# Routed experts in slots of two experts with 64 rows each, their weights copied ahead, in place of slots of one expert with 128 rows

## The chip, the cores and the metric

The kernel runs on one core of one Trainium2 chip. The metric is device time in microseconds of one execution of the whole program, as the median of several runs. The program is one block of instructions for each of the five engines (TensorE or PE, VectorE or DVE, ScalarE or ACT, GpSimd or POOL, and SyncE or SP, which only issues DMAs), tied together by semaphores written by hand.

## The reference

A stack of layers over an input of 4 x 512 tokens of 128 features, all fp32: a linear recurrence, two layers of local attention with a gated feed-forward, a global attention with 8 heads, and last a mixture of experts. Only the last part is touched. With 2048 tokens `x`, 32 experts of hidden size 256 and a shared expert:

```
chosen = the expert with the highest gate logit of the token (one per token), score s
h      = normed token, scaled by s
routed = (silu(h @ Wg[chosen]) * (h @ Wu[chosen])) @ Wd[chosen]     # 128 -> 256 -> 128
out    = x + shared_expert(normed token) + routed
```

How many tokens an expert gets is known only when the kernel runs, so rows are sorted by expert on the chip.

## The kernel before, in words

**Sorting.** VectorE counts the tokens of each expert, and gives each expert as many tiles of P = 128 rows as it needs. `ntile` is the number of tiles (a comparison of the count with 0, 128, 256, ..., one column for each of the TILES = 16 possible tiles, on 32 x 16 = 512 elements, L1191, and its sum, L1193), `incl` its running sum, `base_e` the first tile of each expert. From these comes `slot_i`, the row of `xs_dram` of each token, and semaphore `slots` releases POOL, which scatters the 16 tiles of 128 token rows (129 values: 128 features and the token's number) with 16 indirect DMAs (L645). A table `exp_of` then names the expert of each tile (L1209 and L1211, on one partition, 52 x 32 = 1664 elements). Meanwhile the shared expert runs on TensorE, ScalarE and VectorE; its last add (L1110) brings semaphore `x4s` to 4. `xs_dram` was filled with zeros earlier, in one DMA beside the first layers.

**The slots.** In the worst case there are 16 + 31 = 47 tiles, rounded to LOOP_TILES = 48 slots; all are always run. Slots run in a software pipeline: `experts` emits four slots, a hardware loop (`Fori`) of 10 passes with four slots, and four more; so semaphore targets and addresses in the loop come from registers. Slot j does this:

- SP loads its 128 rows from `xs_dram` into one of four buffers, `rows_in` (L508, `refill`). A refill waits for the transposition of the tile that was in the buffer and for its number.
- POOL takes the token numbers out of the rows (`number`, L653) into `slot_id`. Empty rows are sent to one of four spare rows of `y_dram`.
- PE transposes the rows (`tokens_T`, L1596), ACT brings them to SBUF (`tokens_sb`, L839).
- PE reads the expert's number into a register (`expert_of`, L1599, a value load out of `exp_of`), then multiplies: rows stationary, the expert's gate and up weights moving, 512 columns, straight out of `wgu`, in which all 32 experts lie (`gate_up`, L1603). An fp32 matmul is two instructions here.
- ACT makes Silu of the gate half (`gate_sb`, L845), DVE multiplies it with the up half (`gated`, L1222).
- PE transposes the product in two pieces (`gated_T`, L1609), ACT brings it back (`back_sb`, L851), PE multiplies it with the down weights in `wd` (`down`, L1616, two matmuls of 128 columns).
- DVE copies the result to `ys` (L1231), and POOL scatters its 128 rows to their places in `y_dram` with one indirect DMA (L670). Before the number of slot j+2, POOL waits until the scatter of slot j-2 has landed (`ys_out`).

On each engine the stages are offset: in step j PE does gate-up of j+2, the tokens' transposition of j+3, the product's transposition of j+1 and down of j.

**The end.** SP waits for the scatters, gathers `y_dram` in token order in four DMAs, DVE adds them (L1240), SP writes the output.

Of the kernel before, what the change touches and what calls it, by code (L numbers as in the profile page):

```python
# [8 lines left out]
I32 = mybir.dt.int32  # L9
U32 = mybir.dt.uint32  # L10
ALU = mybir.AluOpType
# [3 lines left out]
P = 128  # L15
# [52 lines left out]
def build(nc, A, out):  # L68
    with ExitStack() as ctx:
# [137 lines left out]
        m3 = region_r[0:1, 3072:3072 + (LOOP_TILES + AHEAD) * EXP]  # L207
# [11 lines left out]
        exp_of_f = region_b[0:1, 8800:8800 + LOOP_TILES + AHEAD]  # L219
        exp_of = region_b[0:1, 8864:8864 + LOOP_TILES + AHEAD].bitcast(I32)  # L220
# [12 lines left out]
        def bank(n, width=BANK, of=1):  # L233
# [20 lines left out]
            "sp_turn", "pool_turn", "ids", "xT_mm", "xT_sb", "gu_mm", "r_silu", "r_act", "actT_mm", "actT_sb", "y_mm", "y_sb", "x4")}  # L254
# [4 lines left out]

        def experts(engine, step):  # L260


            for r in range(AHEAD):
                step(0, r, False)
            with engine.Fori(1, PASSES - 1) as i:
                for r in range(AHEAD):
                    step(i, r, False)
            for r in range(AHEAD):
                step(PASSES - 1, r, True)
# [119 lines left out]
        def _(sp):  # L389
# [110 lines left out]
            def refill(t, j):  # L500

                sp.wait_ge(M["xT_mm"], j + 1)
                if not isinstance(j, int):
                    sp.sem_inc(M["sp_turn"], 1)
                sp.wait_ge(M["ids"], j + 1)
                if not isinstance(j, int):
                    sp.sem_inc(M["sp_turn"], 1)
                sp.dma_start(rows_in[t], xs_dram[bass.ds((j + AHEAD) * P, P), :]).then_inc(xs_in[t], 16)  # L508

            def sp_step(i, r, last):  # L510
                if not last:
                    refill((r + NUM) % AHEAD, i * AHEAD + r + NUM)

            for t in range(NUM):
                refill(t, t)
            experts(sp, sp_step)
            for r in range(AHEAD):
                sp.wait_ge(ys_out[r], 16 * PASSES)
# [7 lines left out]
            for r in range(AHEAD):  # L526
                sp.wait_ge(xs_in[r], 16 * (PASSES + (r < NUM)))
# [4 lines left out]
        def _(pool):  # L532
# [115 lines left out]
            def number(t, i):  # L648
# [7 lines left out]
            for t in range(NUM):  # L656
                number(t, 0)
# [1095 lines left out]
```

## Time and profile before

| | |
|---|---|
| runs | 841.93 us median of 3 (841.46 to 844.74) |
| the profiled execution | 842.27 us |
| its span, first to last instruction | 840.5 us |
| mean granted TensorE clock | 0.920 of full speed |
| PE busy / weight loads busy | 664.2 us (79%) / 396.8 us (47%) |
| DVE / ACT / POOL busy | 518.7 (62%) / 374.4 (45%) / 323.9 us (39%) |
| DMA | 50.57 MB, mean 60 GB/s |
| the chain that ended last | PE 48%, DVE 19%, issue 14%, DMA 7%, ACT 7%, POOL 3% |

Busy time is the time in which an engine had at least one instruction in execution; register, branch and semaphore instructions are not in it. They run on an engine's queue and are named with a q (`PEldq`). The chain that ended last goes back from the last instruction, at each step to what released it; "issue" in it is time in which nothing in the profile was waited for. A timeline row gives start, duration, engine, line and operation, out<-in and a count, and in brackets how long the engine had been idle and what ended that.

### The profile page before, as it was taken

What the parts mean: (1) busy time and instruction counts of PE and PEld (TensorE: products, weight loads), DVE (VectorE), ACT (ScalarE), POOL (GpSimd) and SP (SyncE); (2) the same over time, 40 slices, a digit from 0 to 9 for tenths busy, and PEclk for the clock granted to TensorE, in tenths of its full rate; (3) what the DMA queues carried; (4) which work ended last, traced back from release to release, by engine and by line L of the source; (5) the groups of instructions that cost most, each with busy time, mean ns of one, the idle gap of its engine ahead of it and who ended that gap; (6) DMA issues with size and microseconds to landing.
All of it is one profiled execution on the core that took longest, in us unless ns stands there. A gap on an engine that the chain in (4) does not pass through costs nothing.

```text
span 840.5 us, 14653 instructions
## 1 busy us (share of the span) xinstructions
PE 664.2 (79%) x5076; PEld 396.8 (47%) x5078; DVE 518.7 (62%) x915; ACT 374.4 (45%) x602; POOL 323.9 (39%) x318
## 2 busy tenths in 40 slices
PE   3566899999998999999775555789888966888881
PEld 2244666566656656665553232123233544455551
DVE  7647998778778777877733256866763553222222
ACT  0113446756575564657443542254656521333330
POOL 4544556454454445546311063200001017355552
PEclk8659999999999999999998966689999988899996
DMA  8103210100010010001000137636326101122224
GB/s 253 28 13 117 81 27 21 27 21 13 21 28 18 16 27 14 20 21 27 15 1 1 45 79 154 152 100 143 109 79 229 49 4 47 49 62 60 59 60 119
DMA packets 35507, 50.57 MB, mean 60 GB/s; under 512 B 5965, under 2 KB 24697, under 8 KB 34169
## 3 DMA queue, kind: packets, MB, share of 16 engines
q1 hardware_dynamic: 33401, 45.58, 20.9%
q0 software_dynamic: 2048, 4.21, 1.5%
q8 instruction: 38, 0.62, 0.3%
q14 instruction: 20, 0.16, 0.1%
HBM read 30.31 MB, written 11.83 MB: 50 GB/s over the span
## 4 chain that ended last, share of the span: by engine, by line
PE 48%; DVE 19%; issue 14%; DMA 7%; ACT 7%; POOL 3%; SPq 1%; POOLq 0%; DVEq 0%; ACTq 0%
PE ps L1603 5%; PE ps L1397 5%; DVE region_b L965 5%; DVE smx L962 5%; PE ps L1351 4%; PE ps L1337 4%; PE ps L1308 4%; PE ps L1328 3%; DVE mneg L1139 3%; PE ps L1405 3%; PE ps L1461 3%; DMA region_b<-parts_dram 2%; PE ps L1616 2%; ACT pts L723 2%; PE ps L1545 2%
## 5 line engine op out<-in xcount | busy, mean ns | idle before, releaser
L567 POOL TENSOR_TENSOR rnorm<-ssum_c,neg_half 128x16 f32<-128x16 f32 x32 | 93.8, 2932 | 157.0 <-DVE ssum_c L935 157.0
L1139 DVE TENSOR_REDUCE mneg<-ps 128x2 f32<-128x1024 f32 x64 | 75.3, 1217 | 33.1 <-PE ps L1532 33.1
L579 POOL TENSOR_TENSOR region_r<-region_b,region_d 128x512 f32<-128x512 f32 x64 | 80.8, 1283 | 30.3 <-DVE region_b L940 29.5
L813 ACT ACTIVATE region_r<-ps 128x1024 f32<-128x1024 f32 x64 | 64.4, 1024 | 54.2 <-PE ps L1545 54.1
L545 POOL TENSOR_TENSOR var_eps<-mv,eps 128x4 f32<-128x4 f32 x20 | 5.0, 250 | 184.4 <-DVE mv L878 184.4
L1222 DVE TENSOR_TENSOR region_r<-region_r,ps 128x256 f32<-128x256 f32 x48 | 20.2, 422 | 77.0 <-ACT region_r L845 45.5
L670 POOL DMA_INDIRECT y_dram<-region_r x48 | 50.0, 1043 | 44.3 <-DVE region_r L1231 25.9
L1603 PE MATMUL ps<-region_a,region_r 128*128 x96 | 55.4, 660 | 13.2 <-issue 12.5
L684 ACT ACT_TABLE_LOAD x49 | 62.9, 1283 | 1.6 <-PEq L1745 0.7
L699 ACT ACTIVATE region_a<-ps 128x1024 f32<-128x1024 f32 x32 | 33.0, 1032 | 63.0 <-PE ps L1295 63.0
L1397 PE MATMUL ps<-region_a,region_d 128*114 128x512 f32 x96 | 49.4, 640 | 12.8 <-ACT region_a L717 8.6
L992 DVE SCALAR_TENSOR_TENSOR region_b<-ps,b,region_a 114x512 f32<-114x512 f32 x24 | 18.0, 751 | 53.5 <-ACT region_a L747 53.5
L962 DVE TENSOR_REDUCE smx<-ps 128x8 f32<-128x1024 f32 x32 | 39.2, 1224 | 15.7 <-PE ps L1328 15.3
L1337 PE MATMUL ps<-ident,region_b 128*128 128x128 f32 x256 | 35.0, 280 | 15.3 <-DVE region_b L965 15.3
L1337 PEld LDWEIGHTS ps<-ident,region_b 128*128 128x128 f32 x256 | 27.4, 141 | 40.0 <-DVE region_b L965 40.0
L1294 PE MATMUL ps<-region_d,hT 128*128 128x512 f32 x64 | 36.1, 648 | 11.0 <-DVE region_b L940 7.8
L716 ACT ACTIVATE region_a<-ps 128x512 f32<-128x512 f32 x32 | 19.1, 597 | 57.3 <-PE ps L1308 57.3
L839 ACT ACTIVATE region_r<-ps 128x128 f32<-128x128 f32 x48 | 13.3, 278 | 70.0 <-PE ps L1596 70.0
L932 DVE TENSOR_REDUCE ssum<-region_a 128x16 f32<-128x1024 f32 x32 | 38.8, 1213 | 9.2 <-ACT region_a L699 9.2
L1351 PE MATMUL ps<-region_b,pts 128*64 128x65 f32 x512 | 36.6, 226 | 8.6 <-ACT pts L723 8.5
L940 DVE TENSOR_TENSOR region_b<-ps,rnorm 128x1024 f32<-128x1024 f32 x32 | 39.0, 1218 | 6.0 <-POOL rnorm L567 6.0
L1532 PE MATMUL ps<-region_b 96*128 96x512 bf16 x96 | 34.0, 451 | 9.4 <-DMA region_b<-parts_dram 4.4
(214 smaller groups left out, 1549.9 us busy)
## 6 DMA issues: line engine op xcount, KB each, us to landing
region_a<-in_wgu SPq DMA_DIRECT2D x16, 512.0 KB, 3.7
region_b<-region_a SPq DMA_DIRECT2D x56, 130.0 KB, 2.3
region_d<-in_wd SPq DMA_DIRECT2D x4, 1024.0 KB, 5.8
xs_dram<-region_a SPq DMA_DIRECT2D x1, 3354.0 KB, 12.9
pts<-xs_dram SPq DMA_DIRECT2D x50, 64.5 KB
parts_dram<-region_b SPq DMA_DIRECT2D x8, 384.0 KB, 2.6
region_b<-parts_dram SPq DMA_DIRECT2D x6, 384.0 KB, 6.9
region_d<-in_wqkv SPq DMA_DIRECT2D x2, 768.0 KB, 8.6
```

Of the source, the lines that this page charges most:

```text
L567: g.tensor_tensor(rnorm[:, :], ssum_c[n % 2][:, :], neg_half[:, :], ALU.pow).then_inc(S["rnormed"], 1)
L579: g.tensor_tensor(dst, src, tab, ALU.mult).then_inc(S["rot_bb"], 1)
L670: g.indirect_dma_start(out=y_dram[:, :], out_offset=bass.IndirectOffsetOnAxis(ap=slot_id[:, r:r + 1], axis=0), in_=ys[r], in_offset=None). ...
L684: act_(warm[:, :], ones_f[:, 0:1], function).then_inc(S["warm"], 1)
L813: act_(dst, bank(l1_bank[what, b, i], of=2), ACT.Exp).then_inc(T["ex"], 1)
L962: d.tensor_reduce(smx[n % 2][:, :], sc, AX.X, ALU.max).then_inc(S["smax"], 1)
L965: d.tensor_tensor(sdiff[n % 2], sc, smx[n % 2][:, :].unsqueeze(2).to_broadcast([P, HEADS, P]), ALU.subtract).then_inc(S["diffed"], 1)
L1139: d.tensor_reduce(mneg[b % 2][:, 2 * i:2 * i + 2], bank(l1_bank[what, b, i], of=2) .rearrange("p (q t) -> p q t", q=2), AX.X, ALU.max, neg ...
L1337: last = tr(bank(6 + h // 4)[:, (h % 4) * P:(h % 4 + 1) * P], sdiff[n % 2][:, h, :], ident[:, :])
L1351: last = mm(ps[w * WIN:(w + 1) * WIN, c0:c0 + VW], pts[n % 2][:, j, w * WIN:(w + 1) * WIN], vals[:, t, h, :], start=True, stop=True)
L1397: last = mm(ps[0:HW, (6 + g) * BANK:(7 + g) * BANK], w1[k // BATCH][:, g, c, :], hnT, start=True, stop=True)
L1603: mm(bank(2 + t % 2), xsT[t % 2], wgu[:, bass.ds(e, 1), :].rearrange("p a n -> p (a n)"), start=True, stop=True).then_inc(M["gu_mm"], 1)
```

## The change

The unit of sorting becomes HALF = 64 rows. HALVES = 32 is the largest number of halves of an expert, and with 31 more for the split ones there are 63, in PAIRS = 32 slots of two halves, which may belong to two experts. All 32 are unrolled, so targets and addresses are constants, but for the expert's number.

- Sorting: the comparison and its sum run over 32 x 32 = 1024 elements, the table over 64 x 32 = 2048. `xs_dram` has 4096 rows instead of 6656.
- Per slot DVE copies the gate-up weights of the first expert and the down weights of both into SBUF buffers (`weights_one`), ACT copies the gate-up weights of the second (`weights_two`). Three buffers for gate-up, four for down. DVE reads two expert numbers per slot, ACT one; PE reads none.
- PE: `gate_up` is two matmuls, each with 64 of the slot's rows stationary and its own expert's 512 columns moving, into partitions 0 to 63 and 64 to 127 of one bank; `down` is four of 128 columns in the same manner.
- DVE and ACT wait for `slots`, `x4s` and the weights before the first copies; PE's own waits for them go (all but `x4s`).
- POOL, SP: the same steps without the loop.

```diff
-SLOT_TILES = TILES + EXP - 1
-AHEAD = 4
-LOOP_TILES = -(-SLOT_TILES // AHEAD) * AHEAD
-PASSES = LOOP_TILES // AHEAD
-UP, XT, BACK, NUM = 2, 3, 1, 2
-SLOT_ROWS = (LOOP_TILES + AHEAD) * P
+HALF = P // 2
+HALVES = TOK // HALF
+PAIRS = -(-(HALVES + EXP - 1) // 2)
+AHEAD, NUM, GBUF, DBUF = 4, 2, 3, 4
+SLOT_ROWS = PAIRS * P
...
+            for j in range(PAIRS - AHEAD):
                 sp.wait_ge(M["xT_mm"], j + 1)
                 sp.wait_ge(M["ids"], j + 1)
+                sp.dma_start(rows_in[j % AHEAD], xs_dram[(j + AHEAD) * P:(j + AHEAD + 1) * P, :]).then_inc(xs_in[j % AHEAD], 16)
...
+            def number(j):
+                pool.wait_ge(xs_in[j % AHEAD], 16 * (j // AHEAD + 1))
+                if j >= AHEAD:
+                    pool.wait_ge(ys_out[j % AHEAD], 16 * (j // AHEAD))
+                g.tensor_scalar(slot_id[:, j % AHEAD:j % AHEAD + 1], rows_in[j % AHEAD][:, P:ROW], float(j % AHEAD), None,
                                 ALU.max).then_inc(M["ids"], 1)
+            for j in range(PAIRS):
+                if j + NUM < PAIRS:
+                    number(j + NUM)
+                pool.wait_ge(M["ids"], j + 1)
+                pool.wait_ge(M["y_sb"], j + 1)
                 g.indirect_dma_start(out=y_dram[:, :],
...
+            def expert_two(j):
+                return a.value_load(exp_of[0:1, 2 * j + 1:2 * j + 2], min_val=0, max_val=EXP - 1)
+            def weights_two(j, e):
+                need(a, M["gu_mm"], j - GBUF + 1)
+                act_(gu_pair[j % GBUF][1], wgu[:, bass.ds(e, 1), :].rearrange("p a n -> p (a n)"), ACT.Copy)\
+                    .then_inc(M["w_two"], 1)
...
+            for j in range(PAIRS):
+                if j + 3 < PAIRS:
+                    weights_two(j + 3, e)
+                if j + 4 < PAIRS:
+                    e = expert_two(j + 4)
+                if j + 2 < PAIRS:
+                    gate_sb(j + 2)
+                if j + 3 < PAIRS:
+                    tokens_sb(j + 3)
+                if j + 1 < PAIRS:
+                    back_sb(j + 1)
...
-            link(d.tensor_tensor(m1.rearrange("p (e k) -> p e k", e=EXP), cnt.unsqueeze(2).to_broadcast([P, EXP, TILES]),
-                                 consts[:, EXP:EXP + TILES].unsqueeze(1).to_broadcast([P, EXP, TILES]), ALU.is_gt))
+            link(d.tensor_tensor(over, cnt.unsqueeze(2).to_broadcast([P, EXP, HALVES]),
+                                 consts[:, EXP:EXP + HALVES].unsqueeze(1).to_broadcast([P, EXP, HALVES]), ALU.is_gt))
...
+            def experts_of(j):
+                return [v.value_load(exp_of[0:1, 2 * j + w:2 * j + w + 1], min_val=0, max_val=EXP - 1) for w in range(2)]
+            def weights_one(j, pair):
+                need(v, M["gu_mm"], j - GBUF + 1)
+                d.tensor_copy(gu_pair[j % GBUF][0], wgu[:, bass.ds(pair[0], 1), :].rearrange("p a n -> p (a n)"))
+                need(v, M["y_mm"], j - DBUF + 1)
+                for w in range(2):
+                    last = d.tensor_copy(d_pair[j % DBUF][w], wd[:, bass.ds(pair[w], 1), :, :].rearrange("p a c n -> p (a c n)"))
+                last.then_inc(M["w_one"], 1)
...
+            v.wait_ge(M["slots"], 2)
+            v.wait_ge(M["x4s"], BATCH)
+            v.wait_ge(M["w_gu"], 16 * 16)
+            v.wait_ge(M["w_d"], 4 * 16)
+            for j in range(3):
+                weights_one(j, experts_of(j))
+            pair = experts_of(3)
+            gated(0)
+            gated(1)
+            for j in range(PAIRS):
+                if j + 3 < PAIRS:
+                    weights_one(j + 3, pair)
+                if j + 4 < PAIRS:
+                    pair = experts_of(j + 4)
+                if j + 2 < PAIRS:
+                    gated(j + 2)
+                routed_sb(j)
...
+            def gate_up(j):
+                pe.wait_ge(M["xT_sb"], j + 1)
+                pe.wait_ge(M["w_one"], j + 1)
+                pe.wait_ge(M["w_two"], j + 1)
+                for w in range(2):
+                    rows = slice(w * HALF, (w + 1) * HALF)
+                    last = mm(bank(2 + j % 2)[rows, :], xsT[j % 2][:, rows], gu_pair[j % GBUF][w], start=True, stop=True,
+                              skip_group_check=True)
+                last.then_inc(M["gu_mm"], 1)
...
+            def down(j):
+                pe.wait_ge(M["actT_sb"], j + 1)
+                need(pe, M["y_sb"], j - 1)
                 for c in range(IC):
+                    for w in range(2):
+                        at = c * P + w * HALF
+                        last = mm(bank(6 + j % 2)[w * HALF:(w + 1) * HALF, 0:P], actT[j % 2][:, at:at + HALF],
+                                  d_pair[j % DBUF][w][:, c * P:(c + 1) * P], start=(c == 0), stop=(c == IC - 1),
+                                  skip_group_check=True)
```

## Rows read from the trace of the kernel before

**Rows 1.** The chain of waits from 640 us on: start, duration, what.
```profile
714.34 2.11 DMA pts<-xs_dram
...
717.48 2.07 PE ps L1603 x2
...
817.22 3.26 DMA y_dram<-region_r
...
827.53 3.10 DMA y_dram<-region_r
```

**Rows 2.** Groups from 700 us on: count | busy us, mean ns | idle before, releasers.
```profile
L1603 PE MATMUL ps<-region_a,region_r 128*128 x96 | 55.4, 660 | 13.2 <-issue 12.5 <-ACT region_r L839 0.5
L670 POOL DMA_INDIRECT y_dram<-region_r x48 | 50.0, 1043 | 44.3 <-DVE region_r L1231 25.9 <-issue 10.5 <-DMA y_dram<-region_r 4.9
...
L1222 DVE TENSOR_TENSOR region_r<-region_r,ps 128x256 f32<-128x256 f32 x48 | 20.2, 422 | 77.0 <-ACT region_r L845 45.5 <-issue 22.2 <-PE ps L1609 9.3
...
L845 ACT ACTIVATE region_r<-ps 128x256 f32<-128x256 f32 x48 | 18.1, 378 | 2.4 <-PE ps L1603 2.4
...
L1231 DVE COPY region_r<-ps 128x128 f32<-128x128 f32 x48 | 13.6, 284 | 1.3 <-issue 0.8 <-PE ps L1616 0.5
...
L839 ACT ACTIVATE region_r<-ps 128x128 f32<-128x128 f32 x48 | 13.3, 278 | 70.0 <-PE ps L1596 70.0
```

**Rows 3.** Timeline of TensorE, 784 to 800 us.
```profile
787.48 1.12 PE L1603 MATMUL ps<-region_a,region_r 128*128 x2 [0.36 <-issue]
788.44 0.27 PE L1596 MATMUL ps<-ident,pts 128*128 128x128 f32 x1
...
788.76 0.61 PE L1616 MATMUL ps<-region_d,region_r 128*128 x4
789.21 1.07 PE L1603 MATMUL ps<-region_a,region_r 128*128 x2
...
797.92 1.07 PE L1603 MATMUL ps<-region_a,region_r 128*128 x2
```

**Rows 4.** All instructions of line 1599 (the value load): duration ns min/median/max.
```profile
L1599 PEldq FUSED_REGOPS  x122: 46/151/165, 717.0 to 820.0; - x122
L1599 PEldq TENSOR_LOAD <-region_b x72: 296/303/498, 716.5 to 819.6; - x72
```

**Rows 5.** Timeline of POOL, 700 to 840 us.
```profile
725.37 1.05 POOL L670 DMA_INDIRECT y_dram<-region_r  x1 [8.24 <-DVE region_r L1231]
...
820.77 0.21 POOL L653 TENSOR_SCALAR region_r<-pts 128x1 uint32<-128x1 f32 x1 [0.65 <-DMA y_dram<-region_r]
821.61 1.05 POOL L670 DMA_INDIRECT y_dram<-region_r  x1 [0.62 <-issue]
```

**Rows 6.** Timeline of TensorE in the two attentions, matmuls on array quarters and halves.
```profile
559.67 1.07 PE L1461 MATMUL ps<-region_r,pts 128*32 128x512 f32 x8
560.66 0.60 PE L1532 MATMUL ps<-region_b 96*128 96x512 bf16 x2
...
304.56 0.24 PE L1351 MATMUL ps<-region_b,pts 128*64 128x65 f32 x1 [0.42 <-ACT pts L723]
...
305.49 0.22 PE L1351 MATMUL ps<-region_a,pts 128*64 128x65 f32 x1
```

**Rows 7.** All instructions of lines 986 and 803, copies within SBUF.
```profile
L986 DVE COPY region_b<-y x4: 293/295/296, 113.7 to 354.4; 128x256 f32<-128x256 f32 x4
...
L803 ACT ACTIVATE region_b<-pts x8: 629/629/630, 493.6 to 534.7; 128x512 bf16<-128x512 f32 x8
```

**Rows 8.** Timeline of VectorE, 684 to 726 us.
```profile
685.84 0.69 DVE L1193 TENSOR_REDUCE region_b<-region_r 128x32 f32<-128x512 f32 x1
...
696.00 1.87 DVE L1209 TENSOR_TENSOR region_r<-region_r,region_b 1x1664 f32<-1x1664 f32 x1
...
714.57 0.69 DVE L1110 TENSOR_TENSOR xr<-xr,ps 128x512 f32<-128x512 f32 x1 [4.82 <-remote]
720.38 0.42 DVE L1222 TENSOR_TENSOR region_r<-region_r,ps 128x256 f32<-128x256 f32 x1 [5.13 <-ACT region_r L845]
```

More of the change, by code:

```diff
@@ L258, in build @@
         block = ctx.enter_context(nc.Block())
[L260 to L269, printed above, removed]
         def l1_steps():
@@ L498, in _ @@
                 sp.dma_start(rows_in[r], xs_dram[r * P:(r + 1) * P, :]).then_inc(xs_in[r], 16)
-            def refill(t, j):
+            for j in range(PAIRS - AHEAD):
                 sp.wait_ge(M["xT_mm"], j + 1)
-                if not isinstance(j, int):
-                    sp.sem_inc(M["sp_turn"], 1)
                 sp.wait_ge(M["ids"], j + 1)
[L506 to L516, printed above, removed]
+                sp.dma_start(rows_in[j % AHEAD], xs_dram[(j + AHEAD) * P:(j + AHEAD + 1) * P, :]).then_inc(xs_in[j % AHEAD], 16)
             for r in range(AHEAD):
-                sp.wait_ge(ys_out[r], 16 * PASSES)
+                sp.wait_ge(ys_out[r], 16 * (PAIRS // AHEAD))
             for b in range(BATCH):
@@ L832, in _, with tokens_sb @@
                 silu(n)
[L834 removed]
+            def expert_two(j):
[4 more added lines that the diff above has]
+                    .then_inc(M["w_two"], 1)
+            def tokens_sb(j):
                 a.wait_ge(M["xT_mm"], j + 1)
[L837 to L839 removed]
@@ L841, in gate_sb @@
-            def gate_sb(t, j):
+                need(a, M["gu_mm"], j - 1)
+                act_(xsT[j % 2], bank(j % 2)[:, 0:P], ACT.Copy).then_inc(M["xT_sb"], 1)
+            def gate_sb(j):
                 a.wait_ge(M["gu_mm"], j + 1)
-                if not (isinstance(j, int) and j < 2):
-                    a.wait_ge(M["r_act"], j - 1)
-                act_(silu_r[t % 2], bank(2 + t % 2)[:, 0:INTER], ACT.Silu).then_inc(M["r_silu"], 1)
-            def back_sb(t, j):
+                need(a, M["r_act"], j - 1)
+                act_(silu_r[j % 2], bank(2 + j % 2)[:, 0:INTER], ACT.Silu).then_inc(M["r_silu"], 1)
@@ L848, in back_sb @@
+            def back_sb(j):
                 a.wait_ge(M["actT_mm"], j + 1)
-                if not (isinstance(j, int) and j < 2):
-                    a.wait_ge(M["y_mm"], j - 1)
-                act_(actT[t % 2], bank(4 + t % 2)[:, 0:INTER], ACT.Copy).then_inc(M["actT_sb"], 1)
-            def act_step(i, r, last):
-                for lag, do in ((XT, tokens_sb), (UP, gate_sb), (BACK, back_sb)):
-                    if not last or r + lag < AHEAD:
-                        do(r + lag, i * AHEAD + r + lag)
@@ L858, in _ @@
-            for t in range(XT):
-                tokens_sb(t, t)
-            for t in range(UP):
-                gate_sb(t, t)
-            back_sb(0, 0)
-            experts(a, act_step)
+                need(a, M["y_mm"], j - 1)
+                act_(actT[j % 2], bank(4 + j % 2)[:, 0:INTER], ACT.Copy).then_inc(M["actT_sb"], 1)
+            a.wait_ge(M["slots"], 2)
+            a.wait_ge(M["x4s"], BATCH)
+            a.wait_ge(M["w_gu"], 16 * 16)
+            weights_two(0, expert_two(0))
+            tokens_sb(0)
@@ new lines, in down @@
+                last.then_inc(M["y_mm"], 1)
+            pe.wait_ge(M["x4s"], BATCH)
+            tokens_T(0)
+            tokens_T(1)
+            gate_up(0)
+            tokens_T(2)
+            gate_up(1)
+            gated_T(0)
+            for j in range(PAIRS):
+                if j + 2 < PAIRS:
+                    gate_up(j + 2)
+                if j + 3 < PAIRS:
+                    tokens_T(j + 3)
+                if j + 1 < PAIRS:
+                    gated_T(j + 1)
+                down(j)
```

125 lines of the change are left out of this document (38 added, 87 removed).

## The prediction

> **What bounds the kernel now.** I read the chain of waits first, then the groups of instructions of the last stage, then timelines of single engines. The chain says what the end hangs on: the row loads out of `xs_dram` land at 716.5 us, then TensorE is the chain for most of the stage, then the scatters of the expert rows to `y_dram`, whose last one is under way from 827.53 for 3.10 us, then the four gathers and adds [rows 1]. So the part that the change rewrites runs from 716.5 to 830.6 us: 114 us for 48 slots. All before 690 us, and the last 9.9 us (830.6 to 840.5), are untouched.
>
> In that stage no engine is full: POOL's 48 scatters take 50.0 us, TensorE's gate-up matmuls 55.4 us, VectorE and ScalarE under half of the time [rows 2]. The matmul timeline shows the rhythm: gate-up starts at 789.21 and, four slots on, at 797.92, 2.18 us a slot. A slot without idle takes 1.73 us (787.48 to 789.21: 0.96 for gate-up, 0.32 for three transposes, 0.45 for down) [rows 3]. The other 0.45 us are TensorE's queue: it reads the expert's number into a register 72 times in 48 slots, with a TENSOR_LOAD of 0.303 us each and 122 register operations of 0.151 [rows 4]: 0.303 + 122/72 x 0.151 = 0.56 us a load, about 0.6 with the gaps, 1.5 loads a slot, partly hidden behind matmuls.
>
> POOL stands just behind. A scatter starts only when the one two slots earlier has landed: starts at 817.22 and 821.61 [rows 1, 5], a ring of 4.39 us for two slots, 2.2 us a slot. In it are 3.26 us until the data has landed, 0.29 until the number of a later slot starts at 820.77, and 0.84 from there to the next scatter. So two limits of 2.2 us a slot lie on each other, and the measured 2.18 shows that the coupling of the engines adds nothing visible.
>
> **Part 1, 32 slots for 48.** Every slot still moves 128 rows in and 128 rows out. Sixteen of them go. At today's 2.18 that is -34.9 us. What matters now is the new length p of a slot.
>
> **Part 2, TensorE.** Its value loads all go. Gate-up becomes two fp32 matmuls of 512 columns, each with 64 rows stationary on one half of the array's columns; down becomes four of 128 columns for two. Do the halves run beside each other? Two rows say yes. In the attention, four fp32 matmuls of 512 columns, each on a quarter (`128*32 128x512 f32 x8`, two instructions each), go by in 0.99 us (559.67 to the next start at 560.66), where a single full-width one takes 0.96. And the 32 instructions on halves of L1351 start within 0.93 us, 304.56 to 305.49, 0.03 us each [rows 3, 6]. So a slot stays at 0.96 + 0.32 + 0.45 = 1.73 us. The changes between whole and half array, twice a slot, have no clean row; bound 0 to 0.2 each (idle of that size would still show in rows 6), I take 0.1: TensorE needs 1.9, between 1.7 and 2.2.
>
> **Part 3, VectorE.** It copies one expert's gate-up weights (128x512) and both down weights (128x256 each) in every slot, beside its product (0.422) and its eviction (0.284) [rows 2]. The nearest row for a copy within SBUF is L986, 128x256 in 0.295, against 0.422 for a product of the same size: a copy runs at well above the product's rate [rows 2, 7]. Estimate for 128x512: 0.295 + 256 x 0.52 ns (half of the 1.05 that 0.69 and 0.422 us for 512 and 256 elements make) = 0.43; lower end that, upper end 0.69 (the one-element rate of L1193 [rows 8]). Sum 0.43 + 2 x 0.295 + 0.422 + 0.284 = 1.73, with 0.2 for the gaps of five instructions 1.9 us. It also does two value loads a slot, 1.2 us of its queue. They stand behind the three copies, which are issued first and run for 1.02 us meanwhile; then comes the product, which needs the gate's Silu anyway. Hidden fully: 1.9. Not hidden at all: 3.1. I take 2.1, since TensorE's queue hides most of its loads the same way. New waits of VectorE (gate-up of j, down of j-1) name work that is done before its previous eviction, and cost nothing; if they were late, gate-up of the next slot would be.
>
> **Part 4, ScalarE.** One copy of 128x512; the nearest row, SBUF to SBUF, is L803 with 0.629 [rows 7]; with Silu 0.378, the other 128x256 eviction about the same and 0.278 [rows 2] it is 1.66 us a slot plus one value load, mostly beside it: 1.7 to 2.3. In front of nothing critical; if it lost its cover, Silu and so VectorE's product would be late.
>
> **Part 5, POOL and SP.** Same scatter, same number, same waits in the same order: the ring of 2.2 us stays (the lesser register work is worth nothing inside a ring made of a landing). SP's refill waits on the same two events, and a load is asked for four slots ahead.
>
> So TensorE 1.9, VectorE 2.1, ScalarE 2.0, ring 2.2. I start from p = 2.2 and add a third of the price below for POOL being disturbed: **p = 2.35**.
>
> What a row shows first: the copies of L986 take 0.295 us where a one-element rate gives 0.422 [rows 2, 7], and no row has POOL start a scatter beside one. The Trainium skill, "SBUF — State Buffer", "SBUF: two separate sides", says that such an fp32 SBUF-to-SBUF copy of VectorE shuts GpSimd off its shared port, so that it can't write the descriptors of its own DMAs. By that rule the ring would stretch as the second rival works out; without it p is 2.2. No run here shows it yet.
>
> **Part 6, before the loop.** "More than" over 1024 elements instead of 512, and its sum: L1193 takes 0.69 for 512 and L1222 0.422 for 256 [rows 8, 2], so 1.22 for 1024, +0.53 each, +1.1 us ahead of the row scatters and of the shared expert. The expert table grows from 1664 to 2048 elements: L1209's 1.87 becomes 2.3, and its sum likewise, +0.9. Both lie ahead of the shared expert's last add on VectorE (714.57 [rows 8]), whose chain with TensorE and ScalarE has no slack; it ends 1.9 us later, at 717.2. Only then do the copies begin: two value loads (1.2) and three copies (1.1), so the first weights stand at 719.5, where gate-up started at 717.5 (its chain row [rows 1]). VectorE then prepares slots 1 and 2 and reads pair 3 (three times about 1.6) before the first product: at 724.4 instead of 720.38 [rows 8]. The first scatter follows 5.0 us after the first product today [rows 5, 8], with three slow gate-ups on the way (the first took 2.07 us [rows 1]); they are done by then, so I take it at 729 instead of 725.37 (+3.6, bounds +2 and +6). Zeroing less of `xs_dram` lies beside the layers, worth nothing.
>
> **The sum.** First scatter 729.0; 31 more starts at p; last landing 3.1; tail 9.8: a span of 741.9 + 31p. At p = 2.35 that is 814.8. The profiled execution was 842.27 us at a span of 840.5, 1.8 outside it: **816.5 us**. The median of the three runs (841.93) is 0.3 below the profiled one, less than I can tell. The span equals today's at p = 3.18; 0.5% (4.2 us), about what this measurement can tell from no change, is reached at p = 3.03 and 3.30.
>
> **Rivals.**
> 1. Leaner than thought, p of 2.05 to 2.15 (two scatters of the ring overlap better once the row latencies fall): 807 to 810 us. Chance 0.08. Against it: the ring is a landing, which the change does not touch.
> 2. VectorE's copies disturb POOL. POOL's part of the ring that could be stopped is number, start-up and descriptor work, 0.84 + 1.04 = 1.9 us in two slots; a copy runs 1.02 of every 2.2 us, so about 0.46 of it falls on copies, 0.9 us in two slots, p = 2.65: 825.9 us. With part of the value loads exposed on top, up to p = 3.0 and 837 us. For it: the copies are certain and POOL's ring has no slack. Against it: VectorE copies right after its eviction, while POOL needs some 0.75 us before its scatter starts, so much of the lock would fall in a pause. Chance 0.20.
> 3. VectorE's value loads take the place of TensorE's. If its queue does not read registers while its copies run, each slot costs 1.9 + 2 x 0.6 = 3.1 us, and 3.4 with 0.75 a load. Time 839.8 to 849: the other side of today. It decides from a slot of 3.18 us on. Against it: TensorE has slots of 1.73 us without idle, with a load inside [rows 3]. No change 0.05, slower 0.05 (the next one's share is in neither).
> 4. The halves do not run beside each other, so the change doubles TensorE's work instead of sharing it: 1.92 + 0.32 + 0.90 = 3.14 us a slot, 3.3 with the mode changes: 841 to 846 us. [rows 6] speak against it. Chance 0.02.
>
> **How the numbers follow.** The forecast, p between 2.15 and 2.55 (810 to 823 us), has 0.60. Faster by over 0.5%: 0.60 + 0.08 + 0.20 = 0.88; within 0.5% 0.05; slower 0.05 + 0.02 = 0.07. The range goes from 808 (rival 1 in large part) to 834 (rival 2 but for its end); it leaves out some 0.17.
>
> **What would show it.** 32 scatters with starts 2.2 to 2.5 us apart, and 4.4 or more for two; TensorE's two gate-up halves starting together, next start within 1.1 us; VectorE copies near 0.43 and 0.295 (0.69 would mean that the fast copy is not in use); its value loads in the copies' shadow; the first scatter near 729. A scatter instruction longer than 1.05 us, or the 0.84 us before it grown, shows rival 2; VectorE idle for "issue" before its product shows rival 3; gate-up of 1.9 us shows rival 4. I am wrong if p is outside 2.15 to 2.55, or if the first scatter comes after 731.

## The result and the profile after

| | before | after |
|---|---|---|
| median of four runs | 842.42 us (841.46 to 844.74) | 804.56 us (803.24 to 806.3) |
| profiled execution, span | 842.27, 840.5 us | 806.3, 804.5 us |

The ratio is 0.9547, with an interval of 0.9523 to 0.957: 38 us or 4.5% faster. The prediction said 816.5 us, 808 to 834. So the direction was right and the size too small; the result lies 3.4 us below the range.

The page of the kernel after, its span and first part:

```profile
span 804.5 us, 14011 instructions
...
PE 640.2 (80%) x5125; PEld 369.6 (46%) x5125; DVE 532.3 (66%) x979; ACT 378.5 (47%) x586; POOL 309.2 (38%) x286
```

Its groups from 700 us on (columns as in rows 2):

```profile
L1613 PE MATMUL ps<-region_b,region_r 128*64 128x512 f32 x128 | 35.0, 626 | 0.0
L639 POOL DMA_INDIRECT y_dram<-region_r x32 | 33.2, 1039 | 20.2 <-DVE region_r L1226 9.9 <-POOL region_r L629 9.7 <-issue 0.6
L1630 PE MATMUL ps<-region_b,region_r 128*64 128x128 f32 x256 | 20.9, 285 | 0.0
L807 ACT ACTIVATE region_b<-region_a 128x512 f32 x32 | 19.9, 622 | 6.6 <-DVE xr L1096 6.2 <-issue 0.4
...
L1214 DVE COPY region_b<-region_d 128x256 f32 x64 | 15.8, 287 | 0.0
L1220 DVE TENSOR_TENSOR region_r<-region_r,ps 128x256 f32<-128x256 f32 x32 | 13.5, 421 | 19.5 <-issue 9.9 <-PE ps L1620 6.3 <-ACT region_r L819 3.2
L1211 DVE COPY region_b<-region_a 128x512 f32 x32 | 13.4, 420 | 3.3 <-issue 3.3
...
L629 POOL TENSOR_SCALAR region_r<-pts 128x1 uint32<-128x1 f32 x32 | 12.4, 387 | 6.5 <-DMA pts<-xs_dram 3.8 <-issue 0.9 <-DMA y_dram<-region_r 0.9
```

Gate-up, which in [rows 2] had 13.2 us of idle time in front of it, now has 0.0: TensorE is never idle just before gate-up or down. The matmul timeline of the kernel after shows a rhythm without a gap:

```profile
758.00 1.03 PE L1613 MATMUL ps<-region_b,region_r 128*64 128x512 f32 x4
758.96 0.33 PE L1604 MATMUL ps<-ident,pts 128*128 128x128 f32 x1
759.12 0.38 PE L1620 MATMUL ps<-ident,region_r 128*128 128x128 f32 x2
759.43 0.66 PE L1630 MATMUL ps<-region_b,region_r 128*64 128x128 f32 x8
759.92 1.03 PE L1613 MATMUL ps<-region_b,region_r 128*64 128x512 f32 x4
```

From start to start: 0.96 for both halves of gate-up (one expert alone took 0.96 before), 0.47 for three transposes (0.32 in [rows 3]), 0.49 for both halves of down (0.45), 1.92 us a slot. POOL keeps up with it; its timeline (the answer to [rows 5]):

```profile
732.24 1.05 POOL L639 DMA_INDIRECT y_dram<-region_r  x1 [7.49 <-DVE region_r L1226]
...
757.80 1.04 POOL L639 DMA_INDIRECT y_dram<-region_r  x1 [0.36 <-POOL region_r L629]
758.88 0.60 POOL L629 TENSOR_SCALAR region_r<-pts 128x1 uint32<-128x1 f32 x1
759.67 1.04 POOL L639 DMA_INDIRECT y_dram<-region_r  x1 [0.20 <-POOL region_r L629]
760.75 0.59 POOL L629 TENSOR_SCALAR region_r<-pts 128x1 uint32<-128x1 f32 x1
761.54 1.05 POOL L639 DMA_INDIRECT y_dram<-region_r  x1 [0.20 <-POOL region_r L629]
...
784.14 0.41 POOL L629 TENSOR_SCALAR region_r<-pts 128x1 uint32<-128x1 f32 x1 [0.42 <-DMA y_dram<-region_r]
```

Two slots take 3.74 us here (757.80 to 761.54) where [rows 1, 5] gave a ring of 4.39, and the number at 760.75 starts without a wait for the scatter of 757.80. Only near the end (784.14 and 788.24) does the profile name a landing as what POOL waits for. Three more numbers (743.71, 753.08 and 776.48) follow 0.3 us of idle time that is put down to issue, and each starts 3.2 us behind a scatter with 107 to 115 empty rows (counted as told under "The landing"); these were probably short waits for a landing too. The end of the chain of waits:

```profile
791.56 3.10 DMA y_dram<-region_r
...
796.26 4.68 DMA region_b<-y_dram
```

**Where the time went.** Each profile can be cut at three events of POOL's timeline: the first row scatter (into `xs_dram`), the first result scatter (into `y_dram`) and the last one. The table gives the first, the distance to the second, the mean spacing of the result scatters, and what follows after the last one starts.

| profile | span | first row scatter | to first result scatter | spacing | last start to end |
|---|---|---|---|---|---|
| before | 840.5 | 691.40 | 33.97 | 2.174 x 47 | 13.0 |
| after | 804.5 | 698.41 | 33.83 | 1.913 x 31 | 12.9 |

So the profiled 36.0 us are made of: 16 slots fewer at the old spacing, -34.8; 31 spacings 0.26 shorter, -8.1; a start 7.0 us later; the rest -0.2 (rounded). The tail did not change. TensorE's granted clock is no part of the shorter spacing: it was 1.00 from 730 to 790 us in both profiles.

### The profile page after: what moved, and what is told of

Same layout as the page of the kernel before. It is cut to its first block, busy times and chain, and to the rows that moved or that the text cites. A ratio compares the mean times of both kernels' runs of the same rounds, so it can differ in the third digit from the quotient of the medians.

```text
span 804.5 us, 14011 instructions
## 1 busy us (share of the span) xinstructions
PE 640.2 (80%) x5125; PEld 369.6 (46%) x5125; DVE 532.3 (66%) x979; ACT 378.5 (47%) x586; POOL 309.2 (38%) x286
## 4 chain that ended last, share of the span: by engine, by line
PE 52%; DVE 19%; issue 12%; DMA 6%; ACT 6%; POOL 2%; SPq 1%; POOLq 0%; DVEq 0%; ACTq 0%
PE ps L1405 6%; DVE region_b L951 5%; DVE smx L948 5%; PE ps L1359 5%; PE ps L1345 4%; PE ps L1316 4%; PE ps L1336 4%; PE ps L1613 4%; PE ps L1469 3%; PE ps L1413 3%; DVE mneg L1125 3%; PE ps L1553 3%; DMA region_b<-parts_dram 2%; PE ps L1630 2%; ACT pts L690 2%
## 5 line engine op out<-in xcount | busy, mean ns | idle before, releaser
L1540 PE MATMUL ps<-region_b 96*128 96x512 bf16 x96 | 36.0, 471 | 14.5 <-DMA region_b<-parts_dram 9.7
L1359 PE MATMUL ps<-region_b,pts 128*64 128x65 f32 x512 | 36.5, 225 | 8.8 <-ACT pts L690 8.6
L690 ACT ACTIVATE pts<-ps 128x1024 f32<-128x1024 f32 x32 | 32.7, 1023 | 18.5 <-PE ps L1345 18.5
L639 POOL DMA_INDIRECT y_dram<-region_r x32 | 33.2, 1039 | 20.2 <-DVE region_r L1226 9.9
L1316 PE MATMUL ps<-ident,region_r 128*128 128x128 f32 x256 | 35.4, 283 | 6.2 <-DVE rot_b L888 6.2
L951 DVE TENSOR_TENSOR region_b<-ps,smx 128x1024 f32<-128x1024 f32 x32 | 39.2, 1224 | 1.1
```

The source lines that it names most:

```text
L690: act_(pts[n % 2].rearrange("p h q -> p (h q)"), bank(6, of=2), ACT.Exp).then_inc(S["exped"], 1)
L951: d.tensor_tensor(sdiff[n % 2], sc, smx[n % 2][:, :].unsqueeze(2).to_broadcast([P, HEADS, P]), ALU.subtract).then_inc(S["diffed"], 1)
L1316: last = tr(bank(6 + z)[:, h * P:(h + 1) * P], rot[n % 2][:, (z * HP + h) * P:(z * HP + h + 1) * P], ident[:, :])
L1359: last = mm(ps[w * WIN:(w + 1) * WIN, c0:c0 + VW], pts[n % 2][:, j, w * WIN:(w + 1) * WIN], vals[:, t, h, :], start=True, stop=True)
```

## The experiments

The texts put on record before each run use four letters. Two theories stood at first. **A**: TensorE's queue alone made the 2.18 us of the kernel before, and the scatter ring, read where the slots are empty, is shorter in the body; in the new kernel TensorE sets the slot. **B**, as predicted: the ring of 2.2 us a slot stands whatever TensorE does. Later two more came: **C**, the landing of a scatter depends on how many of its rows go to the same spare row of `y_dram`; and **D**, it has nothing to do with the destinations. Experiments on 48 slots start from the kernel before (b_), those on 32 slots from the kernel after (a_). All but the last two are single executions, beside one or more of the kernel before on the same chip; those of the kernel before alone lie between 841.5 and 845.8 us, so spacings tell more than times.

**b_noload: no value loads on TensorE, loop kept.**

```diff
-                return pe.value_load(exp_of[0:1, bass.ds(i * AHEAD + t, 1)], min_val=0, max_val=EXP - 1)
+                return 0
...
```

> The kernel before, in which TensorE reads no expert number: all 48 slots use expert 0 (left out: the choice of the weights). Theory A: before was bound by TensorE's queue alone, and the scatter ring of 4.39 us for two slots was read where the slots are empty; in the body it is shorter. Then a slot falls from 2.18 us to 1.75 to 1.9, and the span by 14 to 20 us. Theory B, as predicted: the ring of 2.2 us a slot stands whatever TensorE does. Then a slot stays at 2.15 to 2.2 us and the span within 2 us of before.

**b_unroll: the loop written out, the loads kept** (`for i in range(PASSES)` for the hardware loop).

> The kernel before with its hardware loop written out, all register loads kept (six for four slots). Theory A: the loads are what costs, the loop's branch and register arithmetic only a little: a slot of 2.05 to 2.15 us, the span 2 to 6 us less. Rival: the loop costs as much as the loads: a slot of 1.9 us, 13 us less. Theory B (ring of 2.2): nothing.

840.64 and 842.51 us, beside 845.81 for the kernel before. Spacings 2.084 and 2.113 for 2.174: taking every load away gives 0.09 us a slot, the loop alone 0.06. In b_noload the spacing lies between what A said (1.75 to 1.9) and what B said (2.15 to 2.2), so neither holds as it was put; b_unroll came out as A had it (2.05 to 2.15). Without the loads POOL's ring is the main limit. From b_noload, 730 to 826 us, the chain by line, and below it one of the waits (us in total, times, the longest):

```profile
by line: DMA y_dram<-region_r 57.6%; issue 25.2%; DMA pts<-xs_dram 5.8%; POOL region_r L653 3.8%; POOL y_dram L670 3.8%; DVE region_r L1231 1.2%; ACT region_r L845 1.2%; PE ps L1596 1.1%; POOLq L265 0.7%; POOLq L651 0.4%; POOLq L666 0.3%; P
```

```profile
POOL region_r L653 <- DMA y_dram<-region_r: 10.9, 18, 0.9
```

And its DMA issues from 730 to 770 us, with the median time from issue to landing at the end:

```profile
y_dram<-region_r POOLq DMA_INDIRECT x20, 3.0
```

A landing of 3.0 with 0.29 and 0.84 behind it (Part 5's terms) makes 4.1 for two slots, against 2 x 2.084 = 4.17 measured. So TensorE's queue was not the only limit: a ring close to the one of the prediction is there. But the kernel after runs at 1.92 with the same POOL code, so it has to have a shorter ring, and that needs a cause.

**a_serial: the first expert's rows full width.** In gate-up of the kernel after, the first matmul keeps all 128 rows stationary, so it can't run beside the second.

```diff
                     rows = slice(w * HALF, (w + 1) * HALF)
+                    if w == 0:
+                        rows = slice(0, P)
```

> The kernel after, but the first expert's gate-up is a full-width matmul over all 128 rows, and the second's overwrites the upper half; same results. The two can't run beside each other. If they do so in the kernel after, gate-up grows by its whole length, 0.86 us, a slot from 1.92 to 2.8, the span by some 27 us. If the halves ran one after the other anyway, or something other than TensorE set the slot, it grows by less than 0.3 us.

840.15 us, beside 845.81. Its matmul timeline:

```profile
759.20 2.13 PE L1615 MATMUL ps<-region_b,region_r 128*128 128x512 f32 x4
761.26 0.33 PE L1604 MATMUL ps<-ident,pts 128*128 128x128 f32 x1
761.43 0.38 PE L1622 MATMUL ps<-ident,region_r 128*128 128x128 f32 x2
761.74 0.66 PE L1632 MATMUL ps<-region_b,region_r 128*64 128x128 f32 x8
762.33 2.13 PE L1615 MATMUL ps<-region_b,region_r 128*128 128x512 f32 x4
```

Gate-up takes 2.06 for 0.96 and the slot 3.13 for 1.92, more than the 2.8 that was expected (the profiled span grew by 34 us for 27). Of the 1.21 us, 0.96 are work that no longer runs side by side; the other 0.25 are a remainder, which I put down to two more changes between whole and half array in each slot (within gate-up, and ahead of it). The side-by-side run of the halves is what the change lives on: without it 32 slots cost about what 48 did.

**a_nocopy: VectorE's three copies cut to one column each, from slot 4 on.**

```diff
-                d.tensor_copy(gu_pair[j % GBUF][0], wgu[:, bass.ds(pair[0], 1), :].rearrange("p a n -> p (a n)"))
+                n = 1 if j >= DBUF else 512
+                d.tensor_copy(gu_pair[j % GBUF][0][:, 0:n], wgu[:, bass.ds(pair[0], 1), 0:n].rearrange("p a n -> p (a n)"))
...
```

> The kernel after, where from the fifth slot on VectorE's three weight copies are one column each (left out: the weights of the first expert and of down; the slots then use old ones). Theory A: TensorE sets the slot: it stays at 1.90 to 1.93 us. Rival: VectorE sets it: 1.85 or less. If VectorE's copies hold POOL's port, POOL's number instruction (0.39 us in the mean after, 0.22 before) goes back to 0.22, and scatter starts no longer coincide with the end of the second down copy; if not, both stay.

802.98 us, spacing 1.914, as A said; the kernel after, run again later, had 802.77. POOL's timeline of a_nocopy, and one of its groups:

```profile
756.40 1.04 POOL L639 DMA_INDIRECT y_dram<-region_r  x1 [0.55 <-POOL region_r L629]
757.48 0.24 POOL L629 TENSOR_SCALAR region_r<-pts 128x1 uint32<-128x1 f32 x1
758.26 1.05 POOL L639 DMA_INDIRECT y_dram<-region_r  x1 [0.55 <-POOL region_r L629]
```

```profile
L1216 DVE COPY region_b<-region_d 128x1 f32 x56 | 5.8, 144 | 0.0
```

The copies do disturb POOL: beside them its number instruction takes 0.60 and 0.59 us, here 0.24. But from the start of the number to the start of the scatter it is 0.78 us in both (757.48 to 758.26; 760.75 to 761.54 above, 0.79), so the longer instruction only fills a gap that is there without it. Starts are 1.86 us apart here and 1.87 there, and the whole spacing is 1.914 and 1.913. One thing limits what this shows of the scatter instruction: in the kernel after it starts as VectorE's last copy ends (759.67 and 759.65 us), so in most slots it hardly runs beside a copy at all. In a_nocopy the two no longer coincide, as expected for a held port.

**The landing.** The landing of the last slot's scatter, whose rows hold no token, takes 3.10 to 3.15 us in every kernel that sends all 128 empty rows to one spare row. Counted from the reference's inputs, the kernel before needs 38 slots of 48 and leaves 74 of 128 rows empty in each of them on average; the kernel after needs 50 halves, 25 slots of 32, with 46 empty rows each. Theory C says that this is what shortened the ring. Its first test is to give each empty row a spare row of its own:

```diff
+SPARE = AHEAD * P
...
-        y_dram = nc.dram_tensor("y_dram", (AHEAD + TOK, P), FP).ap()
+        y_dram = nc.dram_tensor("y_dram", (SPARE + TOK, P), FP).ap()
...
-                g.tensor_scalar(slot_id[:, t % AHEAD:t % AHEAD + 1], rows_in[t % AHEAD][:, P:ROW], float(t % AHEAD), None,
+                g.tensor_scalar(slot_id[:, t % AHEAD:t % AHEAD + 1], rows_in[t % AHEAD][:, P:ROW], spare[:, t % AHEAD:t % AHEAD + 1], None,
...
+        "spare": (P * np.arange(AHEAD)[None, :] + np.arange(P)[:, None]).astype(np.float32),
...
```

**b_noload_spread** is b_noload with this edit, **b_spread** the kernel before with it alone. **b_one** is the kernel before, written out, with one value load per slot in place of 1.5 (the number is kept until down); **b_one_spread** is that with spread spare rows. **a_spread** is the kernel after with spread spare rows.

```diff
-                if r == 0:
-                    held.clear()
...
-                    held[r + UP] = expert_of(r + UP, i)
-                    gate_up(r + UP, i, held[r + UP])
+                    held[i * AHEAD + r + UP] = expert_of(r + UP, i)
+                    gate_up(r + UP, i, held[i * AHEAD + r + UP])
...
```

> The kernel before without TensorE's register loads (expert 0 in all slots, the choice of weights left out), and with the empty rows of a slot sent to 128 different spare rows of y_dram instead of one. Theory C: a scatter's landing, and with it the ring, is long because the empty rows all hit one spare row; then POOL no longer waits for landings, and a slot falls from 2.08 us to POOL's own 1.87, the span from 838.8 to about 829. Theory D: landing has nothing to do with the addresses (only with the rate of the traffic): a slot stays at 2.05 to 2.1 us.

> The kernel before with nothing changed but the spare rows (128 per buffer instead of one). Before took 2.17 us a slot; with TensorE's register loads gone 2.08; with both gone 1.8. If the scatter ring and TensorE's queue were two limits close together, taking the ring away alone leaves TensorE's queue: 2.1 to 2.17 us a slot, and the last landing at 2.2 us instead of 3.1. If the ring was the one limit: 1.9 or less.

> The kernel before with its loop written out and one register load a slot, spare rows as they were: the fourth corner of the square. Two limits close together: the ring holds the slot at 2.05 to 2.1 us although TensorE could do 1.75; if the loads were the one limit, 1.8 to 1.9 us.

> The kernel before with its loop written out, one register load a slot instead of one and a half, and the spare rows spread; all results kept. Theory C: TensorE's queue at about 1.8 to 1.9 and POOL's own 1.87: a slot of 1.87 to 1.95 us, the span near 830, so that about 11 of the 36 us that the change gained are to be had with 48 slots. Theory D: the ring holds it at 2.1 us, the span near 840.

| 48 slots | time | before beside it | spacing |
|---|---|---|---|
| kernel before | 842.27 | | 2.174 |
| b_one, fewer loads and no loop | 841.67 | 842.96 | 2.091 |
| b_noload | 840.64 | 845.81 | 2.084 |
| b_spread, spread rows alone | 841.15 | 842.96 | 2.130 |
| b_one_spread, both | 828.38 | 844.05 | 1.819 |
| b_noload_spread | 826.51 | 844.05 | 1.813 |

Either edit alone gives 1 to 5 us, both together 16 to 18; by 47 spacings, which leave out how late the slots begin, 2 to 4 and 17. That is the mark of two limits that lie on each other. b_spread and b_one came out as expected. The two with both edits went lower than expected (1.87, and 1.87 to 1.95): POOL's own round, which I had taken as 1.87 us, is no floor. What takes over in each single case can be read in the chain by line, 730 to 826 us; this is b_spread's, to be held against b_noload's above:

```profile
by line: PE ps L1605 47.8%; PE ps L1618 22.7%; issue 12.9%; PE ps L1611 10.0%; PE ps L1598 4.8%; POOL y_dram L672 0.9%; DVE region_r L1224 0.5%; ACT region_r L847 0.4%; DVE region_r L1233 0.3%
```

The landings are gone from the chain, and TensorE's matmuls (85%) and the issue time between them are nearly all of it; its timeline still shows the stop before gate-up:

```profile
757.10 0.61 PE L1618 MATMUL ps<-region_d,region_r 128*128 x4
758.15 1.12 PE L1605 MATMUL ps<-region_a,region_r 128*128 x2 [0.43 <-issue]
```

In b_one_spread gate-up starts follow at 1.71 us here, the 1.73 of a slot without idle in [rows 3]; and its last landing, in the chain of waits, is 0.87 us shorter:

```profile
756.61 1.07 PE L1601 MATMUL ps<-region_a,region_r 128*128 x2
...
758.32 1.12 PE L1601 MATMUL ps<-region_a,region_r 128*128 x2
```

```profile
814.21 2.23 DMA y_dram<-region_r
```

C holds for the landing itself: 3.10 with one destination for 128 rows, 2.23 with 128 destinations, with the same 128 rows of 512 bytes.

How it rises in between can be read in the same traces. The landings of all result scatters that the trace of b_noload times, and then of b_spread, shortest, median and longest:

```profile
DMA to landing us min/median/max: 2.3/3.0/3.4
```

```profile
DMA to landing us min/median/max: 2.2/2.3/3.3
```

Set against the empty rows of each slot, counted from the reference's inputs, single landings are:

| empty rows | 0 | 26 or 27 | 77 | 101 to 107 | 125 | 128 |
|---|---|---|---|---|---|---|
| b_noload, one spare row | 2.30 | 2.43 | 2.78 | 2.98 | 3.19 | 3.17 |
| a_serial, one spare row | 2.31 | 2.44 | | 3.07 | | 3.18 |
| b_spread, spread spare rows | 2.31 | | | 2.30 | 2.31 | 2.31 |

Over the 36 landings that b_noload's trace times this is a rise of about 7 ns for each empty row, with a correlation of 0.96; with spread rows nearly every one is 2.31. The mean over slots that hold tokens is 2.88 us in b_noload and 2.64 in a_serial, whose slots are filled like those of the kernel after. With 0.29 and 0.84 behind it, an estimate from these means is a ring of 2.0 us a slot for the old packing and 1.88 for the new one, just under TensorE's 1.92.

> The kernel after with the spare rows spread. TensorE's 1.92 us a slot stay under both theories. Theory C: the landings of the last, empty slots fall from 3.1 to 3.2 us to 2.3 to 2.5; the time from the last scatter's start to the end from 12.9 to 12.2. Theory D: 12.9 stays.

803.62 us beside 844.05. The last landing is 2.23 here too, and the time from the last start to the end falls from 12.9 to 11.9 us (12.2 was expected), but the spacing stays 1.914: in the kernel after the ring no longer binds, so a shorter one gives nothing but the last landing. From its chain of waits:

```profile
789.77 2.23 DMA y_dram<-region_r
```

**a_noload: the kernel after with constant expert numbers,** on VectorE and ScalarE.

```diff
-                return [v.value_load(exp_of[0:1, 2 * j + w:2 * j + w + 1], min_val=0, max_val=EXP - 1) for w in range(2)]
+                return [(2 * j + w) % EXP for w in range(2)]
...
```

> The kernel after, where VectorE and ScalarE take constant expert numbers (left out: the choice of the weights). TensorE sets the slot: 1.92 us stays, and so does the time from the first row scatter to the first result scatter within 1 us, since the first weights are ready before the first rows. Rival: VectorE's loads set the slot: below 1.9, and the first result scatter comes 2 us or more earlier.

802.72 us beside 844.05, spacing 1.902. VectorE's wait before its product, in its timeline of the kernel after and then of a_noload:

```profile
758.29 0.42 DVE L1220 TENSOR_TENSOR region_r<-region_r,ps 128x256 f32<-128x256 f32 x1 [0.49 <-issue]
```

```profile
759.74 0.42 DVE L1220 TENSOR_TENSOR region_r<-region_r,ps 128x256 f32<-128x256 f32 x1 [0.23 <-ACT region_r L819]
```

So of the two loads (taken as 0.6 each from TensorE's in [rows 4]) some 0.5 us stick out behind the copies, and about half of that would be spent on waiting for Silu anyway. VectorE gets through a slot in 1.92 with them, so they cost nothing that the time shows.

**a_again and a_spread5: the kernel after, and a_spread, once more in five rounds** in one session with nine runs of the kernel before (842.96 median).

> The kernel after, unchanged, as the partner of the next run on the same chip: 0.953 to 0.957 of before.

> The kernel after with the spare rows spread. The last landing 0.9 us shorter and TensorE's 1.92 us a slot as before: 0.8 to 1.5 us less than the kernel after in the same call, 0.1 to 0.2%, near what the timing can tell. If the landings mattered in the body as well, 3 us or more.

802.77 us (801.6 to 804.74), ratio 0.953 (0.9509 to 0.955); and 801.89 us (800.38 to 804.66), ratio 0.9516 (0.9491 to 0.954). The spread version is 0.9 us ahead, what its shorter last landing is worth, but the two overlap: it is not told apart.

## Why the prediction was off

**The failed step is Part 5, "the ring of 2.2 us stays".** The 4.39 us were read at 817 to 822 us [rows 1, 5], among the last slots. These hold no tokens, all their 128 rows go to one spare row, and their landing took 3.26 and 3.10 us. I took the landing for a constant of the scatter. It has a part that depends on the destinations: 2.3 us in the loop where they differ, 3.2 where all 128 are the same, and roughly in proportion between. As the change packs the rows better, fewer empty ones travel with each slot, and the ring falls just below TensorE's 1.92. The code of POOL is the same; what it moves is not. That no ring of 2.2 holds in the new kernel is shown by the spacing, 1.913; that the number of equal destinations sets the landing is shown slot by slot. That the ring of the kernel after is 1.88 is an estimate; a_spread, which shortens the landings and leaves the spacing at 1.914, shows that it no longer binds.

**Part 3's 2.1 us for VectorE was too high as well.** With the ring gone it would have been the next limit, and the sum would still have said 808.8 us at p = 2.1. It was 1.9 and 0.2 for value loads that stick out of the copies' shadow. They stick out by 0.5 us, but for about half of that VectorE would wait for Silu anyway, and it kept up with 1.92; without any load the spacing was 1.902. ScalarE's 2.0 did not show either.

**The term on top, a third of a price for POOL being disturbed (p from 2.2 to 2.35), was also wrong in size.** Rival 2's mechanism exists. A number instruction takes 0.387 us on average in the kernel after where the kernel before has 0.21 [rows 5] to 0.24, and a_nocopy takes it back to 0.24. It costs nothing because 0.78 us pass from number to scatter with the copies and without them. The scatter instruction itself stayed at 1.04, but it mostly starts only as the copies end; in a_noload two that ran beside copies for 0.6 to 0.7 us of their length took 1.04 and 1.05, and the longest of a_again and a_spread took 1.10. The Trainium skill, "SBUF — State Buffer", "SBUF: two separate sides", says that whoever holds the shared port first keeps it for its whole instruction. The trace agrees with that for the number (0.60 us beside the copies, 0.24 without them); the warning of the same section of the Trainium skill, that descriptor work starves, did not show on the result scatters.

A longer POOL instruction did show before the loop. From the timelines of the kernel after, VectorE's and then POOL's:

```profile
703.21 2.27 DVE L1196 TENSOR_TENSOR region_r<-region_r,region_b 1x2048 f32<-1x2048 f32 x1
```

```profile
702.44 0.95 POOL L621 DMA_INDIRECT xs_dram<-region_b  x1 [0.30 <-issue]
703.70 2.62 POOL L621 DMA_INDIRECT xs_dram<-region_b  x1 [0.30 <-issue]
```

The row scatter that runs beside the expert table, a product of two SBUF operands on one partition, takes 2.62 us for 0.95, and in the kernel before 2.01, beside 1.87 of L1209 [rows 8]:

```profile
696.70 2.01 POOL L645 DMA_INDIRECT xs_dram<-region_b  x1 [0.30 <-issue]
```

Both scatters end 0.84 us after VectorE's instruction. The length of that instruction is not the cause: the sum over the table that follows, as long but with one input, leaves the scatter beside it at 0.96 us. From the same two timelines:

```profile
705.51 2.27 DVE L1198 TENSOR_REDUCE region_b<-region_r 1x64 f32<-1x2048 f32 x1
```

```profile
706.62 0.96 POOL L621 DMA_INDIRECT xs_dram<-region_b  x1 [0.30 <-issue]
```

The same section of the Trainium skill names an operation with two SBUF inputs as one that holds the port against GpSimd; the trace agrees with that too (2.62 us for 0.95). The held scatter makes the 16 row scatters 0.6 us longer than before: first to last start is 20.85 us (698.41 to 719.26) where it was 20.27.

**Right, by steps.** Part 1: 16 slots at 2.18 are -34.9, and -34.8 at the spacing of the whole loop. Part 2: TensorE needs 1.9, measured 1.92; halves side by side; 0.1 for each change between whole and half array, against remainders of (1.92 - 1.73)/2 = 0.10 and in a_serial 0.25 for two. The Trainium skill, "TensorEngine Tiling (Array Packing)", "Key Properties", says that a change of mode drains the engine; these remainders of about 0.1 agree with it, though nothing else was varied to set them apart. Part 3: copies at 0.43 and 0.295, measured 0.420 and 0.287. Rival 3: 0.5 us of VectorE's loads are exposed, without effect. Part 4: 0.629, measured 0.622. Rival 4: the halves are not serial, and a_serial shows what gate-up alone would have cost so, 840.15 us; the rival, with down serial too, gave 841 to 846.

**Part 6, right in its costs and wrong in its path.** The sorting is as costed: 1.22 us each for L1178 and L1180, 2.27 for the table. From VectorE's timeline of the kernel after:

```profile
691.12 1.22 DVE L1178 TENSOR_TENSOR region_r<-ps,region_r 128x1024 f32<-128x1024 f32 x1
692.37 1.22 DVE L1180 TENSOR_REDUCE region_b<-region_r 128x32 f32<-128x1024 f32 x1
...
720.02 0.69 DVE L1096 TENSOR_TENSOR xr<-xr,ps 128x512 f32<-128x512 f32 x1 [3.92 <-remote]
...
727.22 0.42 DVE L1220 TENSOR_TENSOR region_r<-region_r,ps 128x256 f32<-128x256 f32 x1 [0.69 <-ACT region_r L819]
```

From the end of the shared expert's last add (720.71) to the first product it is 6.5 us, where 7.2 was worked out (717.2 to 724.4), and 5.0 more to the first scatter, where 4.6 was taken. But the add starts 21.6 us behind the first row scatter, where before it stood 23.2 behind: the table's +0.9 was put on a chain "without slack" that had some. So the wait for the rows still hides the new work: the first copies run at 722.44, the first rows land at 723.41, and row scatter to result scatter stayed 33.8 (predicted: 729 - 692.5 = 36.5). Instead the first row scatter came 7.0 us later than in the profile of before, of which the sorting makes 1.1. The rest comes from layers that the change does not touch. The stretch 550 to 650 us of the kernel before and then of the kernel after, with the granted clock behind the counts:

```profile
550.00:650.00 100.00, 88.98 (x614) 32.11 (x611) 61.13 (x84) 58.18 (x62) 2.08 (x4) 0.99 0.48 138
```

```profile
550.00:650.00 100.00, 91.68 (x585) 33.14 (x586) 58.42 (x64) 54.34 (x57) 0.00 (x0) 0.91 0.42 123
```

Of TensorE's two levels (1.2 and 2.4 GHz) the granted clock was almost always the full one in one execution, a mean of 0.99, and less often in the other, 0.91, and fewer matmuls got done (585 for 614). That differs from run to run: a_again, the same kernel as after, starts its row scatters at 694.24 with 0.95 in that stretch, and the profiles of the b_ kernels at 693.9 to 695.2. The profile of before that the prediction was read from was the earliest of all, by 2.5 us. The first result scatter came at 732.24, behind the 731 that was named as a sign of being wrong; a late start of layers that the change does not touch made it so, and in a_again it came at 727.47.

With the measured spacing in the formula as given, 741.9 + 31 x 1.913 + 1.8 = 803.0 us, beside 804.56 and 802.77 measured. So p carries the miss. The low end of the range took 2.05 for the smallest p with 0.08 of chance; it should have gone to TensorE's own 1.9, which the text had worked out: above it stood only a ring that rested on rows of one stretch, and the estimates of 2.1 and 2.0 for VectorE and ScalarE, whose excess was value loads taken as partly hidden.

## What to carry to other kernels

Before a transfer's duration is taken as a constant, ask which data the row was read with: the last slots of a padded loop are its extreme case, and the padding's destinations can set the price. Where two limits lie on each other, taking one away shows almost nothing (1 to 5 us here) and both together show it all (16 us of the 38 could be had with 48 slots by the edits of b_one_spread, which keep all results); so when a profile shows two equal limits, try them as a square of four kernels. Two matmuls on halves of the array's columns ran in the time of one, at about 0.1 us for each change of mode by what was left over, and such a packing also pays by what it does to the padding.

## What the runs showed that I had not expected

- An indirect scatter of 128 rows lands in 3.10 us where all rows have one destination and in 2.23 where each has its own, in kernels of 48 and of 32 slots alike; in the loop it is 3.18 and 2.31, and about 7 ns for each row that shares its destination in between. Why the memory or the queue does this no run here shows.
- VectorE's copies of 0.42 and twice 0.29 us stretch a neighbouring POOL instruction of 0.24 us to as much as 0.60, while result-scatter instructions, few of which run beside them, stay at 1.04. One product of 1.87 or 2.27 us from two SBUF operands on a single partition holds an indirect scatter until 0.84 us after its end, and a sum of the same length with one operand does not.
- The layers ahead of the change end up to 6 us apart between executions (first row scatter at 691.40, and at 698.41 less 1.1 for the sorting), with the granted clock of 100 us of them going from 0.99 to 0.91. For single profiles a comparison must start at an event behind them.
- In the kernel after, POOL's own round without a wait is 1.87 us (1.04 for the scatter, 0.78 from number to scatter), just below TensorE's 1.92. In b_noload_spread the same distance from number to scatter is at times 0.47. What makes it 0.78 was not followed up; if it stays, it is the next limit.
- Not tried: slots that are skipped when no token is in them, and an order of TensorE's work with fewer changes of mode, worth up to 0.19 us in each of the 32 slots for TensorE, but only 0.05 as long as POOL's round stays at 1.87.
